# Cross-attention stage of a four-stage megakernel: first block by quarters, another order in the last output group, and the bias added to the rows inside

## The reference

```python
x = x + jnp.tanh(g_xattn[0]) * _L0_xattn_ref(_layernorm(x), ctx_2048, ...)
# in _L0_xattn_ref, with H = 16 heads of 128 (INNER = 2048), attention within each of 16 sequences of 128:
q = rms_norm(x @ q_w + q_b, nq_s)            # the norm is over all 2048 columns
k_img = rms_norm(img_ctx @ ki_w + ki_b, nki_s)
v_img = img_ctx @ vi_w + vi_b
out = softmax(q k^T / sqrt(128)) v           # the text half of the context is empty here
return out @ o_w + o_b
```

## Time and profile before

| | us |
|---|---|
| median of 3 runs | 2036.48 (2034.74 to 2039.1) |
| profiled execution | 2035.24 |
| span in its profile | 2033.5 |
| TensorE busy | 1915.1 (94%) |
| GpSimd busy | 1117.0 (55%) |
| VectorE busy | 985.3 (48%) |
| ScalarE busy | 753.0 (37%) |
| attention stage | 0 to 897.5 of the span |
| mean granted TensorE clock | 0.976 |

### The profile page before, as it was taken

How to read it: one execution, slowest core, us unless ns; L and a number is a source line. 1 busy time by engine, 2 the same in 40 slices (tenths; PEclk the granted TensorE clock), 3 DMA queues, 4 the chain that set the end, 5 groups by cost and what they waited for, 6 DMA issues and landing times. The chain is left out here.

```text
span 2033.5 us, 29418 instructions
## 1 busy us (share of the span) xinstructions
PE 1915.1 (94%) x10300; PEld 1605.8 (79%) x10300; DVE 985.3 (48%) x1657; ACT 753.0 (37%) x1144; POOL 1117.0 (55%) x996
## 2 busy tenths in 40 slices
PE   6999999999999999979999799999889996899998
PEld 5889888988888888957778599999677774678886
DVE  2447444745465544644343133333778876772111
ACT  3336333544346332732121212121444544443433
POOL 6875588548756786444116845660545434843333
PEclk9999999999999999979999899999899998999999
DMA  4331323224222423323145755431898665330000
GB/s 151 103 115 53 114 94 114 73 68 140 97 85 68 145 83 125 126 96 138 48 150 185 238 168 176 145 123 61 241 242 231 183 181 184 128 115 31 21 21 21
DMA packets 172235, 248.10 MB, mean 122 GB/s; under 512 B 44944, under 2 KB 69520, under 8 KB 172112
## 3 DMA queue, kind: packets, MB, share of 16 engines
q1 hardware_dynamic: 157024, 202.09, 31.5%
q0 software_dynamic: 9472, 34.09, 5.1%
q10 hardware_dynamic: 5616, 10.23, 1.3%
HBM read 179.77 MB, written 66.58 MB: 121 GB/s over the span
## 5 line engine op out<-in xcount | busy, mean ns | idle before, releaser
L257 POOL TENSOR_TENSOR a_w_hl<-a_w_raw,a_w_hl 128x512 fp32r<-128x512 f32 x236 | 312.9, 1359 | 142.8 <-ACT a_w_hl L330 142.8
L455 PE MATMUL a_proj<-a_c_hl,a_w_hl 128*128 128x512 f32 x768 | 179.7, 393 | 22.0 <-DVE a_w_hl L576 20.0
L455 PEld LDWEIGHTS a_proj<-a_c_hl,a_w_hl 128*128 128x128 f32 x768 | 144.1, 189 | 53.5 <-issue 21.5
L455 PE MATMUL a_proj<-a_w_hl,a_c_hl 128*128 128x512 f32 x768 | 181.2, 392 | 0.0
L529 PE MATMUL a_proj<-a_w_hl,a_a_hl 128*128 128x512 f32 x768 | 178.5, 391 | 0.0
L455 PE MATMUL a_proj<-a_a_hl,a_w_hl 128*128 128x512 f32 x768 | 176.4, 390 | 0.0
L330 ACT ACTIVATE a_w_hl<-a_w_raw 128x2048 fp32r<-128x2048 f32 x60 | 114.8, 1913 | 151.0 <-PE a_proj L455 106.7
L356 ACT ACTIVATE a_sq<-a_proj,a_vecs 128x512 f32<-128x512 f32 x128 | 88.1, 690 | 219.5 <-PE a_proj L455 139.1
L2529 POOL TENSOR_TENSOR f_a_hl<-f_act_sb,f_a_hl 128x512 fp32r<-128x512 f32 x64 | 87.2, 1364 | 147.5 <-ACT f_a_hl L2577 147.4
L455 PEld LDWEIGHTS a_proj<-a_a_hl,a_w_hl 128*128 128x128 f32 x768 | 143.6, 188 | 29.7
L529 PEld LDWEIGHTS a_proj<-a_w_hl,a_a_hl 128*128 128x128 f32 x768 | 143.0, 188 | 29.1
(11 more groups left out here) (258 smaller groups left out, 3518.7 us busy)
## 6 DMA issues: line engine op xcount, KB each, us to landing
a_w_raw<-in_a_ki_w SPq DMA_DIRECT2D x16, 1024.0 KB, 5.3
a_w_raw<-in_a_vi_w SPq DMA_DIRECT2D x16, 1024.0 KB, 4.9
a_w_raw<-in_a_q_w SPq DMA_DIRECT2D x16, 1024.0 KB, 4.9
a_w_raw<-in_a_o_w SPq DMA_DIRECT2D x16, 1024.0 KB, 5.4
spare<-in_b_gate_up POOLq DMA_DIRECT2D x32, 352.0 KB, 3.8
l_sorted_rows<-b_zeros SPq DMA_DIRECT2D x39, 256.0 KB, 3.2
spare<-l_sorted_rows SPq DMA_DIRECT2D x39, 256.0 KB, 3.1
l_expert_out<-spare ACTq DMA_DIRECT2D x39, 256.0 KB, 3.5
```

The costliest lines, as they stand in the source:

```text
L257: ins = pool.tensor_tensor(w_hl[:, s, 1, k], w_raw[:, s, k], f32(w_hl[:, s, 0, k]), ALU.subtract)
L455: mm = pe.matmul(proj[:, j, :], left, right, start=(k == 0 and n == 0), stop=(k == KC - 1 and n == 2))
```

## The change

- **Start.** SP first issues, for each of four chunks, the ctx chunk (into a part of `qT`, not yet in use, under the name `first_c`) and the quarter of w0 (own semaphores `first_in[k]`), and only then the three constants, w1 and x. ScalarE rounds ctx chunk and w0 quarter in turn, GpSimd subtracts the ctx chunk, VectorE the w0 quarter (`k_split`, for the last one `w_split`). TensorE's first tile of group 0 waits for each chunk by itself, in every block; in later blocks GpSimd's `w_low` signals `k_split` too.
- **w1 of the first block** is subtracted by VectorE, ahead of its first layer norm, instead of by GpSimd, which waits for it before it goes on.
- **The last output group** goes in the order: tile 0 with quarters 0 to 2, tile 1 with 0 to 2, tile 0 and tile 1 with quarter 3, then tile 2 and tile 3 with all four. So ScalarE rounds quarter 15 ahead of the next block's w0 instead of behind it.
- **The bias**, tanh(g) x o_b, is added to the four row buffers by VectorE in output group 13 (`r_biased`), between the low parts of quarters 7 and 8, instead of to the results. The semaphore `o_scaled` is gone, `o_done` takes its place.

The diff, cut to its core:

```diff
@@ SyncE
+            for k in range(KC):
+                sp.dma_start(first_c[:, k, :], ctx_t[k][0]).then_inc(first_in[k], 16)
+                sp.dma_start(w_raw[:, 0, k], groups[0][:, k, :]).then_inc(first_in[k], 16)
             sp.dma_start(vecs[:], W["vecs"]).then_inc(const_in, 16)
...
-            load_ctx(0, 0, 0)
-            load_ctx(0, 0, 1)
-            load_w(0, 0)
-            load_ctx(0, 0, 2)
-            load_ctx(0, 0, 3)
             load_w(1, 1)
...
                 for j in range(TPB):
-                    sp.wait_ge(o_done, TPB * t + j + 1)
+                    sp.wait_ge(o_done, TPB * t + TPB + j + 1)
@@ GpSimd
             for k in range(KC):
-                c_low(0, k)
-            pool.wait_ge(w_split, 3)
-            w_low(1, 1)
+                pool.wait_ge(c_high, k + 1)
+                pool.tensor_tensor(c_hl[:, 1, k, :], first_c[:, k, :], f32(c_hl[:, 0, k, :]), ALU.subtract)\
+                    .then_inc(c_split, 1)
+            pool.wait_ge(w_split, 4)
@@ ScalarE
-            act.wait_ge(const_in, 16 * 3)
-            act.activation(tg[:], gate[:], ACT.Tanh).then_inc(tg_ready, 1)
...
             for k in range(KC):
-                c_high_part(k // 2 + 1, k)
-            w_high_part(1, 0)
+                act.wait_ge(first_in[k], 32)
+                act.activation(c_hl[:, 0, k, :], first_c[:, k, :], ACT.Copy).then_inc(c_high, 1)
+                act.activation(w_hl[:, 0, 0, k], w_raw[:, 0, k], ACT.Copy).then_inc(first_high, 1)
+            act.sem_inc(w_high, 1)
+            act.wait_ge(const_in, 16 * 3)
+            act.activation(tg[:], gate[:], ACT.Tanh).then_inc(tg_ready, 1)
             w_high_part(1, 1)
...
+                    if i == NW - 2:
+                        a_high_part(4 * (i - O0) + 7)
                     if i != O0 - 1 and (i + 2 < NW or not last):
                         w_high_part(NW // 2 * t + (i + 2) // 2 + 1, i % 2)
-                    if O0 <= i < NW - 1:
+                    if O0 <= i < NW - 2:
                         a_high_part(4 * (i - O0) + 7)
@@ TensorE
                         if i == 0:
-                            pe.wait_ge(o_scaled, TPB * t + j + 1)
+                            pe.wait_ge(o_done, TPB * t + j + 1)
...
                         for k in range(KC):
+                            if i == 0 and j == 0:
+                                pe.wait_ge(c_split, KC * t + k + 3)
+                                if k < KC - 1:
+                                    pe.wait_ge(k_split, (KC - 1) * t + k + 1)
+                                else:
+                                    pe.wait_ge(w_split, NW * t + 3)
...
-                for i in range(O0, NW):
+                for i in range(O0, NW - 1):
                     for k in range(4):
                         project_out(i, k, (0, 1) if i == O0 else (0, 1, 2, 3))
+                for j, parts in ((0, (0, 1, 2)), (1, (0, 1, 2)), (0, (3,)), (1, (3,)), (2, range(4)), (3, range(4))):
+                    for k in parts:
+                        project_out(NW - 1, k, (j,))
@@ VectorE
+            for k in range(KC):
+                dve.wait_ge(first_high, k + 1)
+                ins = dve.tensor_tensor(w_hl[:, 0, 1, k], w_raw[:, 0, k], f32(w_hl[:, 0, 0, k]), ALU.subtract)
+                if k < KC - 1:
+                    ins.then_inc(k_split, 1)
+            ins.then_inc(w_split, 1)
...
+            dve.wait_ge(w_high, 2)
+            for k in range(KC):
+                ins = dve.tensor_tensor(w_hl[:, 1, 1, k], w_raw[:, 1, k], f32(w_hl[:, 1, 0, k]), ALU.subtract)
+            ins.then_inc(w_split, 1)
             dve.wait_ge(const_done, 2)
-            dve.wait_ge(w_high, 1)
-            dve.tensor_tensor(w_hl[:, 0, 1], w_raw[:, 0], f32(w_hl[:, 0, 0]), ALU.subtract).then_inc(w_split, 1)
...
+                    if i == O0 + 1:
+                        for j in range(TPB):
+                            dve.wait_ge(r_in[j], 16 * t + 16)
+                            dve.tensor_tensor(residual[j], residual[j], tg_ob[:], ALU.add).then_inc(r_biased, 1)
                 for j in range(TPB):
+                    dve.wait_ge(r_biased, TPB * t + j + 1)
                     dve.wait_ge(o_ready, TPB * t + j + 1)
-                    dve.wait_ge(r_in[j], 16 * t + 16)
                     dve.scalar_tensor_tensor(residual[j], proj[:, j, :], tg[:], residual[j], ALU.mult, ALU.add)\
-                        .then_inc(o_scaled, 1)
-                    dve.wait_ge(o_scaled, TPB * t + TPB + j + 1)
-                    dve.tensor_tensor(residual[j], residual[j], tg_ob[:], ALU.add).then_inc(o_done, 1)
+                        .then_inc(o_done, 1)
```

More of the change, by code:

```diff
@@ L78, in l0_attention @@
         qT = sb("qT", [P, H, BLK])
+        first_c = qT[:, 0:KC, :]
         v = carry.rearrange("p (n m) -> p n m", m=INNER)
@@ L107, in l0_attention @@
         w_in = [sem(f"w_in{s}") for s in range(2)]
+        first_in = [sem(f"first_in{k}") for k in range(KC)]
+        first_high = sem("first_high")
+        k_split = sem("k_split")
         w_high = sem("w_high")
@@ L148, in l0_attention @@
         o_ready = sem("o_ready")
-        o_scaled = sem("o_scaled")
+        r_biased = sem("r_biased")
         o_done = sem("o_done")
@@ L179, in _ @@
             sp.dma_start(gate[:], W["gate"].to_broadcast([P, 1])).then_inc(const_in, 16)
-            sp.sem_inc(w_split, 2)
-            sp.sem_inc(c_split, 2)
+            sp.sem_inc(w_in[0], 16)
+            sp.sem_inc(c_in[0], 32)
+            sp.sem_inc(c_in[1], 32)
             def load_w(n, i):
@@ L257, in w_low @@
                     ins = pool.tensor_tensor(w_hl[:, s, 1, k], w_raw[:, s, k], f32(w_hl[:, s, 0, k]), ALU.subtract)
+                    if i == 0 and k < KC - 1:
+                        ins.then_inc(k_split, 1)
                 ins.then_inc(w_split, 1)
@@ L270, in c_low @@
                     .then_inc(c_split, 1)
+            pool.sem_inc(c_split, 2)
             for k in range(KC):
-                c_low(0, k)
-            pool.wait_ge(w_split, 3)
-            w_low(1, 1)
+                pool.wait_ge(c_high, k + 1)
+                pool.tensor_tensor(c_hl[:, 1, k, :], first_c[:, k, :], f32(c_hl[:, 0, k, :]), ALU.subtract)\
+                    .then_inc(c_split, 1)
+            pool.wait_ge(w_split, 4)
             def block_of_tokens(t, last):
@@ L435, in project @@
                 def project(i, tiles=range(4)):
-                    pe.wait_ge(w_split, NW * t + i + 3)
+                    if i:
+                        pe.wait_ge(w_split, NW * t + i + 3)
                     w = w_hl[:, i % 2]
@@ L440, in project @@
                     a = a_hl if kind == "q" else c_hl
-                    if i == 0:
-                        pe.wait_ge(c_split, KC * t + KC + 2)
                     if i == AT["q", 0]:
@@ L533, in project_out @@
                             mm.then_inc(o_ready, 1)
-                        elif j == tiles[-1] and 0 in tiles:
+                        elif j == (1 if i == O0 else TPB - 1):
                             mm.then_inc(a_used, 1)
@@ L567, in _ @@
         def _(dve):
-            dve.sem_inc(o_scaled, TPB)
+            dve.sem_inc(o_done, TPB)
+            dve.sem_inc(w_split, 2)
+            for k in range(KC):
+                dve.wait_ge(first_high, k + 1)
+                ins = dve.tensor_tensor(w_hl[:, 0, 1, k], w_raw[:, 0, k], f32(w_hl[:, 0, 0, k]), ALU.subtract)
+                if k < KC - 1:
+                    ins.then_inc(k_split, 1)
+            ins.then_inc(w_split, 1)
             dve.wait_ge(const_made, 3)
```

## The result

| us | before | changed |
|---|---|---|
| median of the first comparison, 4 runs each | 2035.61 (2034.64 to 2039.1) | 2018.69 (2016.61 to 2024.49) |
| its ratio, 95% interval | | 0.9918 (0.9904 to 0.9931) |
| profiled execution, and its span | 2035.24, 2033.5 | 2016.61, 2014.8 |
| end of the attention stage | 897.53 | 883.52 |
| the three stages after it | 1136.0 | 1131.3 |

The change is faster by 16.9 us. The attention stage, the only one that was changed, gave 14.0 us. Another 4.7 us between the two profiled executions lie in stages with the same code. The experiments ask where these come from, and take the 14.0 apart.

A forecast was written before the change was run, and what follows sets the result against it. TensorE was taken to bound the attention stage, so only its idle time could be won. Start 8.85, boundaries 2.7 and end 2.75 less 0.8 at the additions gave 13.5 us gained, forecast 2023.0 us, range 2019 to 2028.5.

The forecast's parts named there:

- a microsecond of scatter: Run-to-run allowance in the range, added to rivals 1 to 3 and the ends of the unknown costs.
- The start (8.85): First block's start: group 1 of matmuls begins at 23.45 us instead of 32.3, 8.85 us gained.
- chain (a): At the start, the path through TensorE's first tiles: group 1 could start at 22.1 us, or 23.9 with slow clock.
- the leading chain: At the start, the later path to group 1: w1, VectorE's split, layer norm and first copy, giving 23.45 us.
- The boundaries (2.7): Three block boundaries: earlier x loads remove TensorE's wait for the first copy, 0.91 us each, 2.7 us gained.
- The additions (-0.8): Bias additions between quarters 7 and 8: quarter 8 comes late, 0.2 us in each of four blocks, 0.8 us lost.
- The end (2.75): Attention stage's end: one VectorE operation follows tile 3's result instead of four pairs, 2.75 us gained.
- 1: Rival at the start: first loads at full pace, w1 by 13.6 us, TensorE's path binds; 2020.8 us, chance 0.20.
- the chain through VectorE: At the start, w1 landing at 15.0 us, its split to 19.3, layer norm, first copy: group 1 at 23.45.
- Rivals 2 to 5: w1 late 2025.9 (0.15); additions late 2025.0 (0.08); start's transfers slow 2041.0 (0.02); start gains nothing 2031.8 (0.02).
- rival 2: At the start, w1 lands as late as before, 17.9 us; total gain 10.6, time 2025.9 us, chance 0.15.

The follow-up runs named there:

- e1: The kernel before, unchanged, traced a second time; 2036.39 us in its one run.
- e2: The changed kernel, unchanged, traced a second time; 2023.11 us against 2037.14 for the kernel before, ratio 0.9931.
- e12: The changed kernel, unchanged, traced a third time; 2023.21 us against 2036.97 for the kernel before, ratio 0.9926.
- e6: Against the kernel before, only the bias added inside, with start and order as before; 2029.74 us in one run.
- e4: The changed kernel with the start undone, keeping the last group's order and the bias inside; 2032.7 us, ratio 0.9981 to the kernel before.
- e5: Against the kernel before, only the last output group's order, quarter 15 rounded ahead of the weights; 2032.66 us in one run.
- e9: The changed kernel with the last output group's order undone, keeping start and bias inside; 2023.63 us, ratio 0.9937 to the kernel before.
- e8: The changed kernel with four more VectorE operations behind the bias additions in output group 13; 2029.43 us in one run.
- e11: The changed kernel with the three constants issued ahead of the first quarters, as before the change; 2021.77 us in one run.
- e10: The changed kernel with the first block's w1 split by GpSimd again, ahead of the first layer norm's power; 2024.89 us in one run.

## Why the prediction was right or wrong

**The range was wrong, by its lower end, and the failed step is the scatter.** The prediction widened its range by "a microsecond of scatter" and took the three later stages at no difference, since nothing in them changes. In the traces these stages took 1131.3 to 1138.0 us with the same code, and 4.7 us less in the changed kernel's first trace than in that of the kernel before. The changed kernel's own runs lay from 2016.6 to 2026.9, and the four of the first comparison drew 2018.69 as their median; eleven further ones came to 2023.1 and 2023.2. The point of 2023.0 is within 0.6 us of the median of all 15, and 4.3 above the one it was compared with. Of these 4.3 us, 0.9 are that the median of the kernel before fell to 2035.61 with a fourth run, and 3.4 that the gain was 16.9. The gain of 13.5 stands against 14.5 over all runs and 14.0 in the stage. The profile of one execution can't show this scatter, but the three runs of the kernel before already lay over 4.4 us, far more than the microsecond allowed.

**The sum came out by some luck.** Between the first two traces the terms are 9.1 at the start, 2.9 at the boundaries, 2.8 at the end and nothing at the additions, 14.8 in all. The stage gave 14.0, since from each block's first turn to the next block's first matmul the changed kernel took 0.74 us longer in all (0.79 between e1 and e2). The prediction has no such term. Its loss of 0.8 at the additions, which did not occur, stood in for it.

**The start (8.85).** 9.1 measured (43.24 - 34.15), and 8.65 by e1 and e2 (43.08 - 34.43). e12 gives less, 7.5: its fourth pair was taken up at 11.78 instead of 10.58, that chunk's matmuls began at 14.36 at the slow pace, and TensorE went on into group 1 without any wait for the copy:

```profile
14.36 21.38 PE L470 MATMUL a_proj<-a_c_hl,a_w_hl 128*128 128x512 f32 x87 [1.01 <-DVE a_w_hl L590]
```

There chain (a) led, and the first turn came 1.1 us after that of e2; w1 landed 0.3 us later there too. Elsewhere the leading chain was named rightly: w1 landed at 14.6 (15.0 forecast), VectorE was free at 19.0 (19.3), group 1 started at 23.13 (23.45), released by L634, the L607 of the kernel before. Two errors cancelled on the way: w1 was issued at 7.41 instead of 5.8, since SP's later issues took up to 0.92 us instead of 0.45, and the transfers then ran faster than I took them. Chain (a) came out near what was worked, by two small errors against each other: pair 0 was taken up at 5.82 (5.2) and the turns were 1.68 us (1.83), so quarter 3's matmuls started at 13.44 (13.2). The pauses between the threes were 0.75 us by the weight loads, not 1 to 2.

**The boundaries (2.7).** The rate of 0.91 each was right and a little low: from a block's first matmul to its first turn the three took 22.94, 22.94 and 22.58 us before and 21.90, 21.91 and 21.76 after, 2.9 in all (2.7 between e1 and e2), and e6, e4 and the full change have no wait there at all. The mechanism was half right. I wrote that the order and the bias together let the x loads out; either suffices, and the order is idle beside the bias (e5, e6, e9).

**The additions (-0.8).** Nil. The four additions took 5.7 us (200.61 to 206.31) where I had 5.9, so quarter 8 was out at 207.0, some 0.6 us before ScalarE saw group 13 end at 207.65; I had put that margin at 0.1 to 0.2 and charged a loss against it. In the first block TensorE took 43.16 us from its last turn in the attention to the next block's first matmul, before and after. The place was rightly named as the tight one (e8, margin 0.4).

**The end (2.75).** Four operations of VectorE fewer behind the last tile, and tile 3's product 2.8 us nearer to the next stage: 6.4 to 3.6. From VectorE's last operation to the next stage it was 2.8 us before (894.01 + 0.69 to 897.53) and after (879.93 + 0.75 to 883.52), as taken.

**The rivals.** 1 came nearest to the first comparison's number (2020.8) and was wrong in its mechanism: w1 landed at 14.6, not 13.6, and the chain through VectorE led. Rivals 2 to 5 fell; w1's landing between 14.5 and 15.2 us in all traces with the new start but e11 leaves nothing to rival 2.

## What to carry to other kernels

When an early start is bought by splitting the first loads, look for the second chain that the first matmuls are not on: here the second weights, the layer norm queued behind them and the first copy decided, and speeding the first tile by 0.8 us brought nothing (in one trace of three the first chain was the slower by a microsecond, so the two are close). Where two edits aim at one wait, try each alone; the cheaper was enough. And set the range of a forecast by the scatter of stages that the change doesn't touch, as well as by the terms of the sum: here it was several microseconds, as much as a third of the gain.

## What the runs showed of the hardware

- An idle stretch of TensorE of 2.0 to 2.3 us inside the attention stage was followed by 1.6 us of slow pace in two of five cases (12.80 us for 48 matmuls in e10, 23.64 for 96 in e8), with a granted clock of 0.50 over 2 us of it, and by none in the other three. After a start from idle the loss varied as well: 23.40, 23.59, 23.97, 24.77 and 24.80 us for the same 96 matmuls in the five traces that start at 20 us; the granted clock reads 1.00 all through those starts, though the pace does not.
- SP's issue of a 256 KB load took 0.38 to 0.43 us for the first five in the changed kernel's traces and 0.85 to 1.07 for the seventh, then 0.43 for the eighth (e11, with the constants ahead: 1.35 for the seventh), so the issue time is not constant.
- VectorE's subtraction of 128 x 512 takes 0.69 us by itself and 1.34 to 1.5 when GpSimd's, which reads two operands, was begun before it. GpSimd's then keeps its 1.26 us.
